# Grouping the value matmuls of an attention pipeline: two bursts of two key chunks a period instead of four bursts of one

## What is computed

```python
scores = jnp.einsum('bhqd,bhkd->bhqk', Q, K) / jnp.sqrt(jnp.float32(dk))
probs = jax.nn.softmax(scores, axis=-1)
intervened = probs.at[:, :, :, 0].set(0.0)
denom = jnp.clip(intervened.sum(axis=-1, keepdims=True), 1e-09, None)
combined = probs + LAMBDA * (intervened / denom - probs)
attn_out = jnp.einsum('bhqk,bhkd->bhqd', combined, V)
...
x = _layernorm(x + attention(x))
x = _layernorm(x + experts(x))
```

## Time and profile before

| | |
|---|---|
| median of 3 runs | 1536.74 us (1535.64 to 1537.03) |
| the profiled execution's own time | 1535.87 us |
| its span, from the first to the last instruction | 1534.1 us |
| attention, with the filling of its pipeline | from 0 to about 990 us |
| the experts | about 1035 to 1480 us |
| mean granted TensorE clock over the span | 0.925 |

### The profile page before, as it was taken

How to read it: one execution, slowest core, us unless ns; L and a number is a source line. 1 busy time by engine, 2 the same in 40 slices (tenths; PEclk the granted TensorE clock), 3 DMA queues, 4 the chain that set the end, 5 groups by cost and what they waited for, 6 DMA issues and landing times. The chain is left out here.

```text
span 1534.1 us, 24265 instructions
## 1 busy us (share of the span) xinstructions
PE 1347.9 (88%) x7048; PEld 581.8 (38%) x7049; DVE 1029.2 (67%) x1877; ACT 811.0 (53%) x1659; POOL 704.6 (46%) x763
## 2 busy tenths in 40 slices
PE   3899999999999999999899999439999999999940
PEld 1233233233233332233233232126666666666630
DVE  6788889888789888889888887343333333333348
ACT  1477576666576676576676676313333333333323
POOL 5214355355345445354454342534444444444457
PEclk7799899999899999899999898759999999999975
DMA  3322132232222222232232210163222222223248
GB/s 99 111 76 88 56 99 74 78 100 68 76 90 83 76 87 86 62 103 72 77 103 64 78 45 10 41 223 41 40 39 42 37 41 42 38 41 41 38 103 238
DMA packets 128546, 115.29 MB, mean 75 GB/s; under 512 B 17616, under 2 KB 114640, under 8 KB 128080
## 3 DMA queue, kind: packets, MB, share of 16 engines
q1 hardware_dynamic: 104640, 96.68, 21.4%
q0 software_dynamic: 23824, 17.61, 7.2%
HBM read 70.41 MB, written 43.81 MB: 74 GB/s over the span
## 5 line engine op out<-in xcount | busy, mean ns | idle before, releaser
L736 DVE TENSOR_REDUCE rowmax_sb<-mx_ps 128x2 f32<-128x1024 f32 x512 | 608.0, 1214 | 110.7 <-PE mx_ps L459 106.8
L621 ACT ACTIVATE probs_sb<-ring_ps 128x512 f32<-128x512 f32 x1024 | 561.0, 598 | 188.7 <-PE ring_ps L470 175.1
L459 PE MATMUL mx_ps<-region_sb 72*128 72x512 bf16 x1024 | 324.9, 400 | 56.4 <-DVE rowmax_sb L736 43.6
L470 PE MATMUL ring_ps<-region_sb 74*128 74x512 bf16 x1024 | 367.3, 393 | 1.4 <-ACT probs_sb L621 1.4
L482 PE MATMUL acc_ps<-probs_sb,values_sb 128*32 128x512 f32 x2048 | 290.7, 642 | 1.0 <-DVE TN_sb L745 0.8
L685 ACT ACTIVATE probs_sb<-ring_ps 128x512 f32<-128x512 f32 x136 | 81.3, 597 | 276.8 <-PE ring_ps L577 276.8
L470 PEld LDWEIGHTS ring_ps<-region_sb 74*128 74x128 bf16 x1024 | 103.6, 102 | 245.7 <-ACT probs_sb L621 124.6
L1032 POOL CAST negmax_parts_sb<-negmax_sb 16x128 bf16<-16x128 f32 x64 | 18.0, 281 | 381.5 <-ACT negmax_sb L627 381.5
L599 PEld LDWEIGHTS mx_ps<-region_sb,probs_sb 128*128 128x128 f32 x1088 | 131.7, 191 | 90.4 <-issue 90.4
L459 PEld LDWEIGHTS mx_ps<-region_sb 72*128 72x128 bf16 x1024 | 95.0, 101 | 185.1 <-DVE rowmax_sb L736 102.5
L1157 POOL DMA_INDIRECT x_d<-probs_sb x68 | 105.5, 1551 | 125.4 <-DVE probs_sb L956 115.1
(11 more groups left out here) (148 smaller groups left out, 1311.0 us busy)
## 6 DMA issues: line engine op xcount, KB each, us to landing
region_sb<-parts_d SPq DMA_DIRECT2D x384, 96.0 KB
probs_sb<-rows_d SPq DMA_DIRECT2D x136, 66.0 KB, 1.8
parts_d<-q_parts_sb SPq DMA_DIRECT2D x16, 384.0 KB, 2.6
parts_d<-k_parts_sb SPq DMA_DIRECT2D x16, 384.0 KB, 2.9
xT_sb<-xT SPq DMA_DIRECT2D x16, 256.0 KB, 3.2
x_sb<-x SPq DMA_DIRECT2D x16, 256.0 KB, 3.1
x_d<-xn_sb SPq DMA_DIRECT2D x16, 256.0 KB, 4.0
y_d<-padrow_sb SPq DMA_DIRECT2D x16, 256.0 KB, 4.3
```

What stands on the lines that cost most here:

```text
L459: last = nc.tensor.matmul(mx_ps[n % 2][:, i, :], QS[b % 2][0:KR, h, P * c:P * (c + 1)], KS[b % 2][0:KR, h, :], start=True, stop=True)
L470: nc.tensor.matmul(bank, KS[b % 2][0:KR + MR, h, P * c:P * (c + 1)], QS[b % 2][0:KR + MR, h, :], start=True, stop=True).then_inc(s_ring_re ...
L621: nc.scalar.activation(PT[u % 2][:, i // QC, i % QC, :], ring_bank("st", u, i), ACT.Exp, scale=SCALE).then_inc(s_ring_done, 1)
L736: V.tensor_reduce(rowmax[u % 2][:, 2 * k:2 * k + 2], mx_ps[n % 2][:, :, :], axis=AXX, op=ALU.max, negate=True).then_inc(s_mx_done, 1)
```

## The change

The `values` calls of key chunks 0 and 1, which stood at steps 1 and 3, now stand together at step 2. Those of chunks 2 and 3, from steps 5 and 7, stand together at step 6. The calls themselves, the waits inside them, and the programs of all other engines stay as they are.

```diff
@@ -533,7 +533,8 @@
                         maxima(p + 2, k)
                     if is_unit(p):
                         scores(p, 2 * k + 1)
-                    if is_unit(p - 1) and k % 2 == 1:
+                    if is_unit(p - 1) and k in (2, 6):
+                        values(p - 1, k // 2 - 1)
                         values(p - 1, k // 2)
                     if k == 1 and is_unit(p + 1):
                         negmax_to_rows(p + 1)
```

## The result

The kernel after takes 1648.86 us (median of 4 runs, 1639.39 to 1656.29), the kernel before 1536.88 in the same comparison: a ratio of 1.071, interval 1.066 to 1.076. The forecast was 1576 us with a range from 1530 to 1611, so the direction was right and the size was not: +112 us instead of +40.

What follows compares the result with a forecast made beforehand. Attention was taken as bound mostly by TensorE, with DVE near its limit and fed through two maxima buffers. The profiled 1535.87 us plus 25 for waits and 15 for the clock gave 1576 us, range 1530 to 1611.

Steps and rivals of the forecast that it cites:

- What bounds the kernel: Attention: TensorE bounds some three quarters, DVE has little slack and bounds g = 0; two maxima buffers link them.
- the first rival: Attention: TensorE's stream decides, the waits don't come, 0.47 us saved a period, 1522 or 1507 us; chance 0.16.
- The waits for DVE: Attention, steps 2 and 6: TensorE waits for reductions, +1.7 us a sequence, +25 us in all, bounds +8 and +35.
- SP and POOL issue what they issued, at times set by the score chunks: SP and POOL in attention: their work is unchanged and its timing follows the score chunks; no cost, no gain.
- The clock: TensorE bursts behind gathered waits at g = 0, 1, 2: half-speed spells, +1.0 us a sequence, +15 us, bounds 0 and +50.
- ACT at nothing: ACT's exponentials in attention: most of the wait for ACT lies inside the wait for DVE, costed at nothing.
- the bound that stood beside the term: ACT's wait in attention, if not hidden inside DVE's: up to 0.2 us a period, 13 us.
- The last rival: TensorE's clock runs away: second long spell in nearly every sequence, about 1611 us, range 1600 to 1630; chance 0.10.

Runs made afterwards that it cites:

- e16: e12 plus exponentials covering half of the queries, so it doesn't compute the layer: 1468.6 us.
- e13: Kernel after with the scatter's first half moved to g = 1 and score matmuls repeated at g = 0, 1 and 2: 1567.77 us, ratio 1.016.
- e7: Kernel after with POOL's four indirect transfers (first half of the scatter) moved from g = 2 to g = 1: 1588.82 us, ratio 1.037.
- e9: Kernel before with the first score matmul repeated at steps 5, 6, 7 of g = 0 and step 1 of g = 3: 1521.92 us, ratio 0.991.
- e15: Kernel before with the scatter's first half moved to g = 1 and score matmuls repeated at steps 5, 6, 7 of g = 0: 1509.85 us, ratio 0.981.
- e4: Kernel after with POOL's three operations on the values moved from g = 2 to g = 3: 1641.22 us, ratio 1.068.
- e3: Kernel after with the first score matmul repeated in TensorE's waits, 22 more matmuls a sequence: 1605.65 us, ratio 1.043.
- e12: Kernel after with the scatter's first half in g = 1 and each maxima reduction reading half of the keys: 1492.5 us.
- e1: Kernel after with only chunks 0 and 1 paired, at step 2; chunks 2 and 3 at steps 5 and 7 as before: 1620.74 us, ratio 1.049.
- e2: Kernel after with only chunks 2 and 3 paired, at step 6; chunks 0 and 1 at steps 1 and 3 as before: 1560.58 us, ratio 1.015.
- e14: Kernel after with DVE's moments and variance operation moved from step 6 to step 7 of g = 2: 1637.93 us.
- e8: Kernel after with DVE's transpose of the sums moved from step 0 of the next period to step 7: 1608.78 us, ratio 1.048.

## Why the prediction was wrong

**What bounds the kernel**, the feed of DVE through two buffers, was right, and so was the first rival's measure of TensorE's saving: 1.86 us for a burst of two, 5.42 for four steps and a burst once nothing else waits (e16).

**The waits for DVE** were right in place, and the periods nearly so in length: steps 3 to 6 at 5.88 us (5.89), g = 2 at 13.95 (13.8), g = 1 at 13.96 (14.3), and g = 3 at 14.85 (15.0) as soon as the scatter stands elsewhere. The four periods of e13 sum to 59.6 us (59.3). But the term was sized too low, and against a sequence of 57.4 us, when the mean of the twelve was 58.4. Against singles with edits of the same kinds, 56.3 us, it is 3.3 a sequence and not 1.7: the kernel before had its own slow spells and a variance operation held by POOL in the number that I took it by.

**The step that failed first** is "SP and POOL issue what they issued, at times set by the score chunks", which put POOL at nothing. POOL's list in g = 2 isn't set by the score chunks but by the output projection, and that stands behind the burst of step 2. The list came 2.5 us later in the period, and DVE's variance operation only 1.6. So it now starts with POOL's first operation on the values and lasts until it ends (1.44 us instead of 0.61), and the reductions behind it come later. With the pair at step 6, exponential 14 comes up to 2.1 us late as well. Moving four transfers, which removed both, gave back 47.5 us of the 90.6, the slow spells that followed included (e7), so this was the largest single part. Not all of it is new: the same move was part of the 8.1 us between e9 and e15, on the kernel before. I had followed the DMAs' waits, but not which of the small operations would now run at the same time.

The Trainium skill ("GPSIMD Engine Reference", Specifications) says that GpSimd shares its SBUF interfaces with VectorE, with contention for VectorE instructions in a 2-port mode or with two SBUF inputs. For the variance operation the trace agrees as far as it goes, with 1.44 us beside POOL's operation and 0.17 once that operation stands elsewhere (e4, e7). Which mode it ran in, the trace doesn't show.

**The clock** was named as a step and mis-sized: +15 us stood there, and repeats of a matmul in the waits brought 43 us (e3) and, once the scatter stood elsewhere, 744.3 - 715.3 = 29 us in the 48 periods (e13 against e7). I had expected the spells at the end of g = 0 and at step 2 of g = 1. They came at the end of g = 0, and at g = 3 behind the waits for DVE and ACT at its start.

**ACT at nothing** holds only while DVE is the slower: with DVE out of the way the ring costs 0.2 us in steps 3 to 6 (e12 against e16), the bound that stood beside the term. In the kernel after it hides behind DVE, so this didn't move the forecast.

**The range** missed because its upper end, 1611, held the waits at +25 us, the clock at its worst (+50) and no unknown cost. Both known terms at their upper bounds would have given 1536 + 35 + 50 = 1621, which the measured time passes too. The last rival (1600 to 1630) came nearest. It had a second long spell in nearly every sequence. That came, at g = 3 and not at g = 1 where I had looked for it, and the rival knew nothing of POOL.

**What stays open** is the lateness of exponential 14: tied to the pair at step 6 and to the transfers' place by e1, e2, e4, e7 and e14, but gone in e8 with both in place. How the 47.5 us of e7 divide between it and the variance operation isn't shown either. Without the long variance operation the 48 periods are 3.5 us shorter (e4) and 15.8 (e14), each with the exponential late and with slow spells of its own.

## What to carry to other kernels

Before grouping work on the engine that feeds others, work out how many steps run without it in between, and hold that against the depth of every buffer behind it: here a saving of 0.47 us a period was lost in two maxima buffers, and with these relieved mostly in three ring banks. Then look at what stands behind the moved work: the output projection came 2.4 us later, an engine with a list of its own came later with it, and two small operations met for longer than before. So read off which small operations meet afterwards. And a wait on TensorE costs more than its length if the clock falls behind it: cheap repeats of a matmul in the waits that can't be avoided made even the kernel before faster, by 1% alone and by 2% with the scatter moved.

## What the runs showed of the hardware

- One burst of column-tiled matmuls costs 0.09 us to enter and about 0.14 to leave beyond its stream: three bursts on end took 2.71 us against 1.00 for one.
- TensorE at 1.2 GHz lasted some 9 us behind waits of 0.99 and 0.47 us with 0.86 us between their ends, and a burst in it took 3.64 instead of 1.92 us. With repeats of a 512-column matmul in the waits the granted clock over 48 periods went from 0.95 to 1.00 on the order of before (e9, e15).
- An operation on 128x4 elements on DVE took 0.17 us alone (e4, e7), 0.61 when it started late in a POOL operation on 128x512 elements (before, e2), and 1.44 when it started with it (after, e1, e8): it ended with POOL's in both.
- An exponential on ACT with its input ready started 0.3 to 2.1 us late in 13 of 16 sequences while POOL issued indirect transfers or had just done so, and on time in all 16 when they were moved (e7). Its cause isn't shown.
